# Key and query products in two float32r parts: two heads on the halves of the array's rows

## What is computed

```python
B, S, D, H, M = (8, 512, 256, 16, 2)     # M modules of H heads, KD = D // H = 16
q  = einsum('btd,mdhk->mbhtk', n1, mha_wq) + mha_bq
kk = einsum('btd,mdhk->mbhtk', n1, mha_wk) + mha_bk
scores = einsum('mbhtk,mbhsk->mbhts', q, kk) / sqrt(KD)
attn = softmax(scores, axis=-1)
ctx = einsum('mbhts,mbhsk->mbthk', attn, v)
```

## Time and profile before

| | |
|---|---|
| median of 3 runs | 1407.55 us (1404.99 to 1409.78) |
| the profiled execution | 1407.98 us, its span 1406.2 us |
| mean granted TensorE clock | 0.995 |
| PE busy | 1380.4 us, 98% |
| DVE busy | 1074.6 us, 76% |
| ACT busy | 911.4 us, 65% |
| POOL busy | 361.0 us, 26% |

### The profile page before, as it was taken

One profiled execution on the slowest core, in us unless ns is written; L12 is line 12 of the kernel. 1 busy time (PEld: TensorE's weight loads), 2 busy tenths in 40 slices (PEclk: granted clock), 3 DMA queues, 4 the chain that ended last, 5 costly groups with the idle time before them and its releaser, 6 DMA issues. The chain is left out here.

```text
span 1406.2 us, 22227 instructions
## 1 busy us (share of the span) xinstructions
PE 1380.4 (98%) x7666; PEld 714.5 (51%) x7666; DVE 1074.6 (76%) x2299; ACT 911.4 (65%) x1708; POOL 361.0 (26%) x351
## 2 busy tenths in 40 slices
PE   8999999999999999999999999999999999999989
PEld 6644445554455544456445654555445555354456
DVE  6789878977698777986879777897779868688631
ACT  3367567756667667776577666775676765657751
POOL 7422341302313223113322034132132222221000
PEclk9999999999999999999999999999999999999999
DMA  4065075321744136530662308441174415352002
GB/s 118 17 79 89 2 79 88 67 55 31 105 62 78 59 44 105 86 55 31 85 96 54 69 16 106 76 76 61 28 109 77 75 31 62 46 69 54 21 12 90
DMA packets 92307, 90.15 MB, mean 64 GB/s; under 512 B 16482, under 2 KB 87266, under 8 KB 91294
## 3 DMA queue, kind: packets, MB, share of 16 engines
q1 hardware_dynamic: 92196, 88.73, 38.1%
HBM read 35.05 MB, written 4.25 MB: 28 GB/s over the span
## 5 line engine op out<-in xcount | busy, mean ns | idle before, releaser
L1710 ACT ACTIVATE prob<-psum 128x512 f32<-128x512 f32 x1024 | 560.6, 600 | 317.9 <-PE psum L910 217.2
L1411 DVE TENSOR_REDUCE mx<-psum 128x1 f32<-128x512 f32 x1024 | 640.6, 681 | 77.8 <-PE psum L880 75.3
L895 PE MATMUL psum<-qst,kst 98*128 98x512 bf16 x1024 | 340.7, 382 | 2.3 <-DMA qst<-mrow 1.3
L880 PE MATMUL psum<-kst,qst 96*128 96x512 bf16 x1024 | 305.1, 381 | 5.5 <-DVE resid L1283 2.2
L910 PE MATMUL psum<-prob,vst 128*17 128x512 f32 x2048 | 246.6, 598 | 0.4 <-ACT prob L1710 0.2
L895 PEld LDWEIGHTS psum<-qst,kst 98*128 98x128 bf16 x1024 | 94.9, 98 | 202.8 <-issue 136.5
L880 PEld LDWEIGHTS psum<-kst,qst 96*128 96x128 bf16 x1024 | 97.5, 97 | 127.7 <-ACT prob L1710 17.1
L1861 POOL CAST parts<-resid 128x512 bf16<-128x512 f32 x64 | 39.4, 616 | 404.0 <-DVE resid L1283 404.0
L910 PEld LDWEIGHTS psum<-prob,vst 128*17 128x17 f32 x2048 | 46.7, 96 | 128.8 <-issue 109.8
L867 PE MATMUL psum<-w,cxT 128*128 128x256 f32 x448 | 105.1, 381 | 0.0
L848 PE MATMUL psum<-n2T,x 128*128 128x512 f32 x224 | 102.0, 592 | 0.0
(11 more groups left out here) (244 smaller groups left out, 1708.3 us busy)
## 6 DMA issues: line engine op xcount, KB each, us to landing
kst<-parts SPq DMA_DIRECT2D x186, 128.0 KB, 4.6
qst<-parts SPq DMA_DIRECT2D x186, 128.0 KB, 5.5
cmat<-G_dram SPq DMA_DIRECT2D x7, 1024.0 KB, 4.7
x<-in_L_ffn_fw SPq DMA_DIRECT2D x14, 512.0 KB, 3.6
w<-in_L_ffn_fw SPq DMA_DIRECT2D x14, 512.0 KB, 4.1
xbuf<-in_x SPq DMA_DIRECT2D x8, 512.0 KB, 5.2
kin<-in_ctx SPq DMA_DIRECT2D x8, 512.0 KB, 4.5
out<-acc SPq DMA_DIRECT2D x7, 512.0 KB, 3.9
```

The lines of the kernel that those rows point to most:

```text
L880: e.matmul(psum[:, u.bank, :], qst[0:KROWS, h, t * P:(t + 1) * P], kst[0:KROWS, h, :], start=True, stop=True).then_inc(u.full, 1)
L895: e.matmul(psum[:, u.bank, :], kst[0:KROWS + 2, h, g * P:(g + 1) * P], qst[0:KROWS + 2, h, :], start=True, stop=True).then_inc(u.full, 1)
L1411: e.tensor_reduce(mx[:, qq * QUAD + j, t:t + 1], psum[:, u.bank, :], AX, ALU.max).then_inc(u.free, 1)
L1710: e.activation(prob[:, g % 2, j, :], psum[:, u.bank, :], ACT.Exp).then_inc(u.free, 1)
```

## The change

K and Q are split in two float32r parts, high (ACT) and remainder (DVE); POOL's part is gone. A head has 3 x 16 = 48 rows (hi*hi, hi*lo, lo*hi) and two for the maximum. Even heads lie on partitions 0 to 49, odd ones on 64 to 113, and a pair of heads goes through the array as two matmuls, one on each half of the rows, into two adjacent banks (`take_two`). One reduction takes the pair's two maxima, one exponential its 1024 columns. The 16 maxima of a quad are copied once more (`mxx`) so that the transpose gives two copies, and the maximum's two rows go by two DMAs, one for each half. The tables of slots are new. The constant ones come out of the bias of ACT's move and one broadcast DMA a half; the router's mean has its own buffers.

```diff
-    TERMS_K = (0, 0, 1, 1, 0, 2)
-    TERMS_Q = (0, 1, 0, 1, 2, 0)
+    TERMS_K = (0, 0, 1)
+    TERMS_Q = (0, 1, 0)
+    HALF = P // 2
+    PAIRS = QUAD // 2
+    UNITS = PAIRS * NT
+    def take_two(self, name, until):
+        k = min(range(self.count - 1), key=lambda k: (max(self.until(k), self.until(k + 1)),
+                                                      max(self.order[k], self.order[k + 1])))
+        self.counts[k] += 1
+        one = self.uses[name] = self.hold(k, self.counts[k], until)
+        one.both = slice(k, k + 2)
+        return one, self.hold(k + 1, one.n, until, k)
...
-        kst = sb("kst", [P, M * H, S], BF16)
+        kst = sb("kst", [P, M * H // 2, S])
...
-        VALUES, COPY, TURN = 1, 3, 7
+        VALUES, COPY, TURN = 0, 3, 7
...
-            AHEAD="1300200300314230044012000010100221221000031300001011000104403001"
-                  "0020100321400001210130341010440001130110030202100012010003000000")
+            AHEAD="1100100001022131101001000001001003001110000110100001000011012020001"
...
             def maximum(b, qq, j, t):
-                u = take("max", b, qq, j, t)
-                e.matmul(psum[:, u.bank, :], qst[0:KROWS, h, t * P:(t + 1) * P], kst[0:KROWS, h, :], start=True,
-                         stop=True).then_inc(u.full, 1)
+                u = take_two("max", b, qq, j, t)
+                for par in range(2):
+                    own = slice(HALF * par, HALF * par + KROWS)
+                    ins = e.matmul(psum[:, u.both, :][:, par, :], qstR[own, h // 2, t * P:(t + 1) * P], kstR[own, h // 2, :],
+                                   start=True, stop=True)
+                ins.then_inc(u.full, 1)
             def score(b, qq, g, j):
-                u = take("score", b, qq, g, j)
-                e.matmul(psum[:, u.bank, :], kst[0:KROWS + 2, h, g * P:(g + 1) * P], qst[0:KROWS + 2, h, :], start=True,
-                         stop=True).then_inc(u.full, 1)
+                u = take_two("score", b, qq, g, j)
+                for par in range(2):
+                    own = slice(HALF * par, HALF * par + KROWS + 2)
+                    ins = e.matmul(psum[:, u.both, :][:, par, :], kstR[own, h // 2, g * P:(g + 1) * P], qstR[own, h // 2, :],
+                                   start=True, stop=True)
+                ins.then_inc(u.full, 1)
...
             def maximum(b, qq, j, t):
-                e.tensor_reduce(mx[:, qq * QUAD + j, t:t + 1], psum[:, u.bank, :], AX, ALU.max).then_inc(u.free, 1)
+                e.tensor_reduce(mx[:, qq, :, j, t], psum[:, u.both, :], AX, ALU.max).then_inc(u.free, 1)
+                if j == PAIRS - 1 and t == NT - 1:
+                    e.wait_ge(u.free, u.n)
+                    src = mx[:, qq].rearrange("p r h t -> p r (h t)")
+                    e.tensor_copy(mxx[:], src.unsqueeze(2).to_broadcast([P, 2, 2, UNITS])).then_inc(maxima_in, 1)
...
-                if q_ > 1:
-                    e.wait_ge(split_lo, q_ - 1)
-                e.scalar_tensor_tensor(out=resid[:, n % 2, :], in0=psum[:, u.bank, :],
+                e.scalar_tensor_tensor(out=partsR[:, n % 2, 1, :], in0=psum[:, u.bank, :],
...
-                e.activation(prob[:, g % 2, j, :], psum[:, u.bank, :], ACT.Exp).then_inc(u.free, 1)
+                e.activation(prob[:, g % 2, 2 * j:2 * (j + 1), :], psum[:, u.both, :], ACT.Exp).then_inc(u.free, 1)
...
-            def middle_low(b, n):
...
             def stack(b, n):
                     for i in range(len(TERMS[which])):
-                        if TERMS[which][i] == j:
-                            e.dma_start((kst, qst)[which][i * KD:(i + 1) * KD, heads, :], parts[:, n % 2, j, :]
-                                        ).then_inc(stacked[which][m][c], 16)
+                        for par in range(2 if TERMS[which][i] == j else 0):
+                            o = HALF * par + i * KD
+                            e.dma_start((kst, qst)[which][o:o + KD, p0:p0 + HP, :],
+                                        parts[HALF * par:HALF * (par + 1), n % 2, j, :]).then_inc(stacked[which][m][c], 16)
```

More of the change, by code:

```diff
@@ L8 @@
 F32 = mybir.dt.float32
-BF16 = mybir.dt.bfloat16
+F32R = mybir.dt.float32r
 U32 = mybir.dt.uint32
@@ L57, in until, with hold @@
         return self.latest[k].until if self.latest[k] is not None else -1000
+    def hold(self, k, n, until, at=None):
+        at = k if at is None else at
+        self.taken += 1
+        self.order[k] = self.taken
+        self.latest[k] = Use(k, n, self.full[at], self.free[at], self.latest[k], until)
+        return self.latest[k]
     def take(self, name, until):
@@ L63, in take @@
         self.counts[k] += 1
[L64 to L68, removed]
+        self.uses[name] = self.hold(k, self.counts[k], until)
+        return self.uses[name]
+    def take_two(self, name, until):
+        assert name not in self.uses
+        k = min(range(self.count - 1), key=lambda k: (max(self.until(k), self.until(k + 1)),
[4 more added lines that the diff above has]
+        return one, self.hold(k + 1, one.n, until, k)
 class Steps:
@@ L478, in take, with take_two @@
                 return u
+            def take_two(*name):
+                both = banks.take_two(name, freed_at(clock[0], *name))
+                for u in both:
+                    if u.was is not None:
+                        e.wait_ge(u.was.free, u.was.n)
+                return both[0]
             def transpose(out_, in_, n):
@@ L887, in max_rows @@
-                src = mx[:, qq * QUAD:(qq + 1) * QUAD, :].rearrange("p h t -> p (h t)")
-                transpose(psum[0:TILES, u.bank, 0:P], src, P).then_inc(u.full, 1)
+                e.wait_ge(maxima_in, b * NQ + qq + 1)
+                transpose(psum[0:2 * TILES, u.bank, 0:P], mxx[:].rearrange("p a r u -> p (a r u)"), P).then_inc(u.full, 1)
             def score(b, qq, g, j):
-                h, q_ = qq * QUAD + j, b * NQ + qq
+                h, q_ = qq * QUAD + 2 * j, b * NQ + qq
                 if g == 0 and j == 0:
@@ L898, in values @@
+                ins.then_inc(u.full, 1)
             def values(b, qq, g):
                 q_ = b * NQ + qq
-                w = uses["score", b, qq, g, QUAD - 1]
+                w = uses["score", b, qq, g, PAIRS - 1]
                 e.wait_ge(w.free, w.n)
@@ L1606, in move_pick @@
                 e.wait_ge(u.full, u.n)
-                e.activation((kst, qst)[which][0:KROWS, h, :], psum[0:KROWS, u.bank, :], ACT.Copy).then_inc(u.free, 1)
+                if which:
+                    e.activation(qstR[:, h, :], psum[:, u.bank, :], ACT.Copy).then_inc(u.free, 1)
+                else:
+                    e.wait_ge(shaped, 3)
+                    e.activation(kstR[:, h, :], psum[:, u.bank, :], ACT.Identity, bias=lift[:]).then_inc(u.free, 1)
             def decays(b):
@@ L1814, in stage_a @@
                 e.tensor_copy(mk[:, b % 2, 1, :], sa.rstd[:, 1, :]).then_inc(kept, 1)
-                for n in range(len(PIECES) // M if b else 3):
-                    yield f"s{n}"
-                    middle_low(b, n)
             def weigh(b):
@@ L2119, in sync_program @@
             a.upto(-9)
-            e.wait_ge(ones, 1)
-            for i in range(1, M * H // HC):
-                e.dma_start(kst[KROWS:KROWS + 2, i * HC:(i + 1) * HC, :], kst[KROWS:KROWS + 2, 0:HC, :]).then_inc(ones_in, 16)
+            e.wait_ge(ones, 2)
+            for par in range(2):
+                own = slice(HALF * par + KROWS, HALF * par + KROWS + 2)
+                e.dma_start(kst[own, HP + 1:M * H // 2, :],
+                            kst[own, HP:HP + 1, :].to_broadcast([2, M * H // 2 - HP - 1, S])).then_inc(ones_in, 16)
             until_maxima(a, first)
```

315 lines of the change are left out of this document (154 added, 161 removed), and 12 rows, old and new, of the table DVE_A.

## The result

The changed kernel takes 1453.59 us (1450.84 to 1455.83, 4 runs), the one before 1408.66 us (1404.99 to 1410.38, 4 runs) beside it: a ratio of 1.032 (95% interval 1.029 to 1.035). It is 45 us slower where I forecast 159 faster, and outside the range. The profiled execution took 1455.83 us, its span 1453.9.

A forecast was written before the change was run, and what follows sets the result against it. PE's matmul stream was taken as the bound. 1406.2 - 219 (pairs) + 52 (shape changes) - 4 (head) + 12 (stalls) = 1247 us of span, plus 1.8: 1249 us. Forecast 1225 to 1275 (chance 0.65); range from 1200 up to 1310.

The forecast's parts named there:

- every change of the array's shape costs about 0.095 us: On PE, 912 changes of shape instead of 364: 548 x 0.095 = plus 52 us, 6.7 in a middle pass.
- My upper bound: High end for the changes of shape on PE: 548 x 0.12 = 66 us; the low end was 0.
- pairs, 1024: PE's scores and maxima: 2048 x 0.217 = 444 us become 1024 x 0.22 = 225, minus 219 us.
- stalls: New waits from first-pass engine balance (5 us) and PE at banks (1 us for each of seven passes): plus 12, between 0 and 50.
- The slow columns: Rival: float32r columns on PE cost the float32 pace, 0.43 us a pair; 1458, or 1470 with stalls; chance 0.06.
- The loads that come out of hiding: Rival: a pair's weight loads on PE can't lie under the pair ahead, 102 us more, 1351; chance 0.04.
- Banks in twos: Rival: DVE and adjacent banks make each pair wait 0.05 us, 51 us instead of 12, 1288 us; chance 0.15.
- The passes: Forecast lengths: middle passes 145 to 147 us, first about 120, last about 115.
- two engines of the same length: First pass: PE 114.6 and DVE 114.8 us can't both be full, so 5 us of stall.
- Head: Opening part: 48 selection matmuls become 16, minus 4 us, between 0 and 8; head 78 us.
- what speaks against the change: The forecast's words for the changes of the array's shape on PE, plus 52 us.
- At nothing: ACT, POOL and SP work, including the pieces' DMAs and the two small ones for the maximum's rows, costed at no time.

The follow-up runs named there:

- the bf16 loop: Row of a separate PE-only program alternating bf16 half-row pairs with a float32 product of 256 columns, data ready and no waits; 0.95 us a round.
- the loops: Separate program of thirteen rows of 12 PE steps, operands in SBUF and no waits, nothing of the kernel computed; float32r pairs in a row take 0.229 us each.
- the expectation's 660: Count of pairs starting right behind their load, stated before running the changed kernel with bf16 instead of float32r parts; that run measured 1378.2 us.
- the bf16 version: The changed kernel with bf16 instead of float32r for K, Q, parts and the maxima's rows, same pairs and order, fewer bits; 1378.2 us, ratio 0.977.
- four buffers: The changed kernel with bf16 parts and four instead of two buffers of exponentials; 1357.11 us, ratio 0.965.
- the unpaired half-row kernel: The kernel before with three of its six products a head (48 and 50 rows), one head after the other; 1509.7 us, ratio 1.074.

## Why the prediction was wrong

**The step that failed first** is "every change of the array's shape costs about 0.095 us", 548 x 0.095 = plus 52. I had read it off two rows with bf16 loads and a short load of 17 columns. Before such a short load a change does cost about that (0.10 us in the bf16 loop). Now the load behind a change has 128 four-byte columns, nothing covers it, and a change costs 0.20. By the loops' prices and the listing's counts: 602 changes between a pair and a float32 product at 0.198, 231 between pairs and values at 0.16 (their loop takes 1.41 us a round, less 0.229 and 0.862 of stream), 79 others at 0.115 make 165 us; the 364 of before at 0.115 are 42. So plus 123 (an estimate), not 52: **71 us** of the miss. My upper bound (0.12 each, 66) came from the same rows, so it bounded the wrong thing.

**The other terms**, each against the span of 1247 us forecast and 1453.9 measured:

| term | forecast | by the runs | missed by |
|---|---|---|---|
| pairs, 1024 | 0.220 us | 0.229 us | 9 |
| changes of shape | +52 | +123 (estimate) | 71 |
| stalls: PE's span less its busy time, 25.8 before, 76.0 after | +12 | +50 | 38 |
| loads behind a late bank | none | 196 x 0.107 = 21 (estimate) | 21 |
| clock: (1 - 0.958) x 1454 less (1 - 0.995) x 1406 | none | up to +54 | 54 |
| sum | | | 193 of 207 |

The loads behind late banks: in the trace 633 of 1024 pairs start within 0.06 us of the start of their own load; 437 of these come behind another kind of row, and 196 behind a pair, whose bank came late (the expectation's 660 counts a few more); a load's exposed part is 0.335 less 0.228. The clock's row is an upper bound, since time at half clock costs only where PE is the bound, and some of it may stand in the stalls as well; so at least 14 us stay open.

**The clock** was in no term. It is told by the last of these rows of the middle pass:

```profile
594.30 1.15 PE L904 MATMUL psum<-kst,qst 48*128 48x512 f32 x4 [0.18 <-DVE mx L1434]
596.09 0.49 PE L904 MATMUL psum<-kst,qst 48*128 48x512 f32 x2 [0.64 <-ACT prob L1745]
596.52 3.59 PE L787 MATMUL psum<-wo,cxT 128*128 128x256 f32 x8
```

The same eight instructions of L787 that took 1.99 us at 607.78 take 3.59 here: the granted clock had gone to the lower of its two levels, 1.2 GHz, behind a stretch of pairs with waits for banks between them. It does so three times in a middle pass at the same places (there 0.97), once in the bf16 version (0.99), and not at all with four buffers (1.00). Where a fall follows waits, the waits cost twice. That they are the cause is not shown: the unpaired half-row kernel has PE busy 99% of its span, and 0.976, and two passes with the same idle time differ in their clock (above). What sets it stays open.

**Rivals.** The slow columns (1458 to 1470) have the time nearly right and the mechanism wrong: a pair takes 0.229 us. The loads that come out of hiding are what happened, in another place than I put them: not under the pair ahead, which hides them, but at each change of shape and each late bank. I had dismissed that rival by the 0.217 us of a maximum, and that row shows a bf16 load in an unchanged shape; it says nothing of either. Banks in twos (0.05 us a pair) happened too: 51 us before 1024 pairs. I took three mechanisms that add up for alternatives, which is why the range ended at 1310. Even added up, by my own prices (102 for the loads, 39 to 61 for the banks), they reach 1390 to 1412: the clock and the waits for the maxima's rows were in none.

**The passes.** Middle 170.7 for 145 to 147: the changes add some 17 us (117 x 0.19 less 46 x 0.115) where I added 6.7, idle time is 5.7 us for 0.2, and the clock up to 5. First 151.9 for 120: I gave it 5 us for two engines of the same length, but its idle time alone grew from 5.4 to 17.4 us, and its clock is 0.91. With DVE's maxima cut short it still takes 146 (clock 0.92), so DVE's length was not most of it. Last 138.3 for 115. Head 81.4 for 78: PE is 4.1 us less busy as forecast, and waits 4.0 longer, at a clock of 0.92 for 0.98.

**What was right:** that halves run side by side in float32r; 1.22 us reductions, 1.14 from one to the next in a row, 1.02 us exponentials, 0.274 us for `mxx`, DVE at 129.7 us a middle pass (131 forecast); the count of changes, and that this is "what speaks against the change"; the pieces' DMAs are little slower (5.0 us from issue to landing, 4.6 before). "At nothing" was not right for the maxima's rows: waits for their DMA and for `mxx` are among the stalls, with 5.8 and 7.2 us.

## What to carry to other kernels

Using half of the array's rows for two products at once pays by the stream (0.217 us saved a pair) and costs at each border with another shape (0.10 to 0.20 us): count the borders by kind in the order as issued and price each with its load, in the type that it will have, before counting what the stream saves. Narrow types pay less at such a border: here bf16 parts took 75 us less than float32r ones with the same pairs, at fewer bits. And when the bound engine gets its work in fewer and larger pieces, its buffers can come back later: look at what holds them (here mostly ACT's exponential of two banks) and at how the order stands to it, since one kind of step moved by one slot cost 89 us.

## What the runs showed that I had not expected

- A load of 128 four-byte columns takes 187 ns by its record, one of bf16 92 to 97; under an unchanged shape both are hidden, even between two pairs that use both halves (0.229 and 0.22 us a pair).
- A float32r instruction over 98 rows fits between float32 products in 0.23 us: 0.67 us a round for the 0.65 of bf16. So float32r is nearly free in a full-row shape, and dear only at changes.
- Twelve float32r matmuls on one half of the rows alone take 3.0 us, as long as twelve pairs, and in the loops the only stretch at a lower granted clock starts right behind them. Together with the unpaired half-row kernel that points at half rows, but no run parts them from the rest, and what sets the clock stays open.

The rows of the last two, from the loops:

```profile
103.00 0.59 PE L56 MATMUL psum<-mr,wr 98*128 98x512 f32 x1
103.43 0.60 PE L56 MATMUL psum<-mf,wf 128*128 128x256 f32 x2
103.67 0.58 PE L56 MATMUL psum<-mr,wr 98*128 98x512 f32 x1
...
114.10 3.01 PE L56 MATMUL psum<-mr,wr 50*128 50x512 f32 x12
117.04 0.56 PE L89 MATMUL psum<-mf,wf 128*128 128x128 f32 x2
117.39 4.41 PE L56 MATMUL psum<-mf,wf 128*128 128x256 f32 x12
```

The twelve instructions of float32 take 4.41 us here and 2.76 in the other places where they stand.
